# One-row DMAs by byte address, shared between SyncE and ScalarE, in the edge gathers of a four-layer graph network

## What is computed

```python
edge_index = jnp.stack([src, dst])
x = _layernorm(x + _L0_gnn_ref(x, edge_attr_2, src, dst, ...))        # softmax over edges, w * (z[src] + ez)
x = _layernorm(x + _L1_gnn_ref(x, edge_index))                        # segment_sum(x[src], dst)
x = _layernorm(x + _L2_gnn_ref(x, edge_index, edge_attr_16, ...))     # attention MLP on every edge, softmax, GRU
x = _layernorm(x + _L3_gnn_ref(x, src, dst, W, b))                    # softmax over edges, h[src] * alpha
```

## Time and profile before

| | us |
|---|---|
| median of 3 runs | 11547.42 (11536.29 to 11568.89) |
| the profiled execution, its time | 11551.36 |
| its span in the trace | 11549.4 |
| POOL busy, share of the span | 8177.0, 71% |
| DVE busy | 5633.5, 49% |
| ACT busy | 2838.7, 25% |
| PE busy | 2429.9, 21% |

### The profile page before, as it was taken

How to read it: one execution, slowest core, us unless ns; L and a number is a source line. 1 busy time by engine, 2 the same in 40 slices (tenths; PEclk the granted TensorE clock), 3 DMA queues, 4 the chain that set the end, 5 groups by cost and what they waited for, 6 DMA issues and landing times. The chain is left out here.

```text
span 11549.4 us, 88417 instructions
## 1 busy us (share of the span) xinstructions
PE 2429.9 (21%) x11904; PEld 1958.6 (17%) x11904; DVE 5633.5 (49%) x13767; ACT 2838.7 (25%) x4017; POOL 8177.0 (71%) x8465
## 2 busy tenths in 40 slices
PE   2322333332000000000000001666666630000000
PEld 2211323222000000000000001555555420000000
DVE  9999888882422222411111112777777642222223
ACT  0165555551211111122222210111111231111111
POOL 0076777777777777777777777777777667777776
PEclk8555555555555555555555555888888755555555
DMA  7011111012222222222222221333333212222222
GB/s 227 11 13 13 13 14 15 7 15 50 64 57 57 55 57 57 49 54 54 53 54 54 54 51 46 86 87 88 86 87 88 64 32 56 55 56 56 56 56 50
DMA packets 711039, 633.45 MB, mean 55 GB/s; under 512 B 476828, under 2 KB 534837, under 8 KB 709423
## 3 DMA queue, kind: packets, MB, share of 16 engines
q0 software_dynamic: 270464, 237.81, 12.7%
q1 hardware_dynamic: 390732, 224.72, 6.9%
q10 hardware_dynamic: 49248, 165.27, 3.7%
HBM read 322.30 MB, written 304.83 MB: 54 GB/s over the span
## 5 line engine op out<-in xcount | busy, mean ns | idle before, releaser
L1235 POOL DMA_INDIRECT l_rows<-table,l_sources x4623 | 4385.9, 949 | 1446.4 <-issue 1409.0
L632 POOL DMA_INDIRECT e_rows<-in_rec,base x1504 | 1530.7, 1018 | 1092.8 <-DVE marks L761 642.7
L1235 POOL DMA_INDIRECT l_pair<-table,l_slab x1568 | 1503.6, 959 | 483.0 <-issue 458.0
L1459 DVE TENSOR_TENSOR_SCAN l_totals<-l_factor,banks 128x510 f32<-128x510 f32 (+3 forms) x672 | 752.6, 1162 | 1638.4 <-ACT banks L1616 1637.4
L1626 ACT COPY l_kept<-l_totals 128x476 f32<-128x476 f32 (+3 forms) x672 | 639.3, 967 | 2990.6 <-DVE l_totals L1459 2980.6
L1390 DVE TENSOR_TENSOR l_score<-l_rows,base 128x14 f32<-128x14 f32 x224 | 44.4, 198 | 2590.4 <-DMA l_rows<-table,l_sources 2590.3
L1576 PE MATMUL banks<-ident,l_kept 128*65 128x128 f32 (+2 forms) x4 | 1.9, 464 | 5756.1 <-DVE junk L1508 5756.1
L1576 PEld LDWEIGHTS banks<-ident,l_kept 128*65 128x65 f32 (+2 forms) x4 | 0.7, 171 | 5758.2 <-DVE junk L1508 5758.2
L779 PE MATMUL banks<-marks 125*128 125x98 bf16 x3200 | 623.3, 366 | 1269.8 <-DVE marks L761 1269.8
L393 DVE COPY_PREDICATED area<-banks,area 128x2048 f32<-128x2048 int32 x342 | 869.4, 2597 | 0.2
L779 PEld LDWEIGHTS banks<-marks 125*128 125x128 bf16 x3200 | 459.9, 148 | 1420.7 <-DVE marks L761 1316.4
(11 more groups left out here) (313 smaller groups left out, 6301.3 us busy)
## 6 DMA issues: line engine op xcount, KB each, us to landing
l_rows<-table SPq DMA_DIRECT2D x6784, 0.3 KB
l_rows<-table,l_sources POOLq DMA_INDIRECT x4623
l_rows<-table SPq DMA_DIRECT2D x3584, 0.2 KB
sums<-l_kept ACTq DMA_DIRECT2D x112, 476.0 KB, 3.0
sums<-l_kept SPq DMA_DIRECT2D x224, 231.0 KB, 3.4
sums<-l_kept ACTq DMA_DIRECT2D x112, 462.0 KB, 2.7
seeds<-late_rows SPq DMA_DIRECT2D x130, 392.0 KB
sums<-l_kept ACTq DMA_DIRECT2D x112, 448.0 KB, 2.6
```

The costliest lines, as they stand in the source:

```text
L632: GP.indirect_dma_start(e_rows[:, u, g, :], None, A["rec16"], bass.IndirectOffsetOnAxis(e_ids[:, s * G16 + g:s * G16 + g + 1], 0)).then_in ...
L1235: GP.indirect_dma_start(pair[:, u, g, 0:D] if gated else rows[:, u, g, :], None, table[l], bass.IndirectOffsetOnAxis(at, 0)).then_inc(rows ...
L1459: V.tensor_tensor_scan(flat(totals[:, s % 2, h, 0:n, :]), flat(factor[:, s % 2, 0:n, :]), flat(fresh[s % 2][h][:, 0:n, :]), 0.0, ALU.mult, ...
```

## The change

One-row DMAs now see table and target as bytes, and their address is a byte offset that needs no scaling by the sequencer: VectorE multiplies the node numbers once by the row's bytes (`alone_wide` for layers 0 and 3, `alone_slim` for 1 and, anew, 2). SP fetches one column in 46 in layers 0, 1 and 3 and, newly, one in 64 in layer 2. ACT, newly, fetches one in 56 in layers 0, 1 and 3: one part of 32 rows in each step, for a column six steps ahead (`ACT_LEAD`). Over the edge loops POOL's columns fall from 1543 to 1510 in layer 0, from 1540 to 1507 in layers 1 and 3, and from 1568 to 1545 in layer 2. `powers_of` and `of_group` take their semaphores from shared ones.

```diff
-            sp.dma_start(alone_ids[0:STEPS // 4 * (P // ALONE_EACH), :],
-                         for_alone[:, :, :, 4 * G - 1]).then_inc(alone_ids_in, 16)
-        ALONE_FIRST = {0: 3, 1: 0, 3: 0}
-        alone_at = lambda l, s: l in ALONE_FIRST and s % 4 == 3 and s // 4 >= ALONE_FIRST[l]
+        SP_STRIDE, SP_FIRST = {0: 46, 1: 46, 2: 64, 3: 46}, {0: 2, 1: 0, 2: 1, 3: 0}
+        ACT_STRIDE, ACT_FIRST, ACT_LEAD = 56, {0: 2, 1: 1, 3: 1}, 6
+        def fetch_row(eng, l, to, at, landed):
+            flat = byte_view(table[l].rearrange("n w -> (n w)"))
+            eng.dma_start(byte_view(to), flat[bass.ds(at, 4 * TWL[l])].rearrange("(o w) -> o w", o=1)).then_inc(landed, 16)
...
+                by_sp = {t: SP_STRIDE[l] * (t + 1) - 1 for t in range(SP_FIRST[l], W // SP_STRIDE[l])} if l in SP_FIRST else {}
+                by_act = {t: ACT_STRIDE * (t + 1) - 2 for t in range(ACT_FIRST[l], W // ACT_STRIDE)} if l in ACT_FIRST else {}
+                alone = set(by_sp.values()) | set(by_act.values())
...
-                        for g in range(cols_by_pool(s)):
+                        for g in range(G):
+                            if s * G + g in alone:
+                                continue
...
+                    if l == 0:
+                        flat = dsrc[0:NQ].rearrange("(i c) -> c i", c=W)
+                        load_places(sp, 0, W // SP_STRIDE[0], flat[SP_STRIDE[0] - 1::SP_STRIDE[0], :])
+                        load_places(sp, ACT_AT, W // ACT_STRIDE, flat[ACT_STRIDE - 2::ACT_STRIDE, :])
...
                     def fetch_alone(s, r, u):
+                        for t, c in by_sp.items():
+                            if gated and 0 <= s - c // G < P // ALONE_EACH:
+                                fetch_part(t, s - c // G)
+                            elif not gated and c // G == s:
+                                if s >= RING:
+                                    sp.wait_ge(*done(read_last, s - RING))
+                                for h in range(P // ALONE_EACH):
+                                    fetch_part(t, h)
-                    in_turn(STEPS, RING, [(0, load), (12, save)] if gated else [(0, fetch_alone)])
+                    in_turn(STEPS, RING, [(0, load), (12, save), (0, fetch_alone)] if gated else
+                            [(0, fetch_alone)])
...
+                    if l == 0:
+                        dve.wait_ge(alone_ids_in, 32)
+                        for q, n in ((0, W // SP_STRIDE[0]), (ACT_AT, W // ACT_STRIDE)):
+                            tl(V.tensor_scalar(alone_wide[q:q + n, :], alone_slim[q:q + n, :], 4.0 * TWL[0], None, ALU.mult))
+                            V.tensor_scalar(alone_slim[q:q + n, :], alone_slim[q:q + n, :], 4.0 * TWL[1], None, ALU.mult
+                                            ).then_inc(alone_scaled, 1)
...
+                    def fetch_alone(s, r, u):
+                        for t, c in by_act.items():
+                            h = s - (c // G - ACT_LEAD)
+                            if 0 <= h < P // ALONE_EACH:
+                                if h == 0 and c // G >= RING:
+                                    act.wait_ge(*done(read_last, c // G - RING))
+                                at = row_places(l, mybir.EngineType.Activation, ACT_AT + t, h)
+                                for i in range(ALONE_EACH):
+                                    p = h * ALONE_EACH + i
+                                    fetch_row(act, l, rows[p:p + 1, c // G % RING, c % G, :], at[i],
+                                              act_rows_in[(t - ACT_FIRST[l]) % 2])
...
-                        in_turn(STEPS, RING, [(1, keep), (1, save), (0, scan_weight)] if soft else
-                                [(0, take_rows), (1, keep), (1, save)])
+                        in_turn(STEPS, RING, [(1, keep), (1, save), (0, scan_weight), (0, fetch_alone)] if soft else
+                                [(0, take_rows), (1, keep), (1, save), (0, fetch_alone)])
```

More of the change, by code:

```diff
@@ L1126, in build, with row_places, load_places @@
         sources_in = sem("sources_in")
-        ALONE_FIRST = {0: 3, 1: 0, 3: 0}
-        alone_at = lambda l, s: l in ALONE_FIRST and s % 4 == 3 and s // 4 >= ALONE_FIRST[l]
-        alone_ids_in = sem("alone_ids_in")
+        SP_STRIDE, SP_FIRST = {0: 46, 1: 46, 2: 64, 3: 46}, {0: 2, 1: 0, 2: 1, 3: 0}
+        ACT_STRIDE, ACT_FIRST, ACT_LEAD = 56, {0: 2, 1: 1, 3: 1}, 6
+        ACT_AT = P // 2
+        alone_ids_in, alone_scaled = sem("alone_ids_in"), sem("alone_scaled")
+        alone_at_byte = [alone_wide, alone_slim, alone_slim, alone_wide]
+        byte_view = lambda a: a.bitcast(mybir.dt.uint8)
+        def fetch_row(eng, l, to, at, landed):
+            flat = byte_view(table[l].rearrange("n w -> (n w)"))
+            eng.dma_start(byte_view(to), flat[bass.ds(at, 4 * TWL[l])].rearrange("(o w) -> o w", o=1)).then_inc(landed, 16)
+        def row_places(l, engine, q, h):
+            _, at = nc.values_load_multi_w_load_instructions(
+                alone_at_byte[l][q:q + 1, h * ALONE_EACH:(h + 1) * ALONE_EACH], [engine], min_val=0,
+                max_val=(NODES - 1) * 4 * TWL[l],
+                skip_runtime_bounds_check_because="source nodes of real and padded places are under NODES")
+            return at
+        def load_places(sp, q, n, words):
+            with nc.allow_non_contiguous_dma(reason="single words of a few columns, once"):
+                sp.dma_start(alone_slim[q:q + n, :], words).then_inc(alone_ids_in, 16)
         def edge_layer(l, k, kind, got, extra=None, first_do={}, node_stage=None):
@@ L1258, in edge_sync @@
                         sp.dma_start(sources[:], dsrc[0:NQ].rearrange("(p c) -> p c", p=P)).then_inc(sources_in, 16)
[L1259 to L1264 removed]
+                    first_do.get("sync", nothing)(sp)
+                    if l == 0:
+                        flat = dsrc[0:NQ].rearrange("(i c) -> c i", c=W)
+                        load_places(sp, 0, W // SP_STRIDE[0], flat[SP_STRIDE[0] - 1::SP_STRIDE[0], :])
+                        load_places(sp, ACT_AT, W // ACT_STRIDE, flat[ACT_STRIDE - 2::ACT_STRIDE, :])
+                    if gated:
+                        flat = rec_s[0:NQ, RE - 1:RE].bitcast(I32).rearrange("(i c) w -> c (i w)", c=W)
+                        load_places(sp, 0, W // SP_STRIDE[l], flat[SP_STRIDE[l] - 1::SP_STRIDE[l], :])
                     if soft:
@@ L1287, in save @@
                                      kept[:, s % KR, :, :]).then_inc(saved[s % KR].sem, 16)
-                    def fetch_alone(s, r, u):
-                        if not alone_at(l, s):
-                            return
-                        if s >= RING:
-                            sp.wait_ge(*done(read_last, s - RING))
-                        for h in range(P // ALONE_EACH):
-                            q = s // 4 * (P // ALONE_EACH) + h
-                            _, at = nc.values_load_multi_w_load_instructions(
-                                alone_ids[q:q + 1, :], [mybir.EngineType.SP], min_val=0, max_val=NODES - 1,
-                                skip_runtime_bounds_check_because="source nodes of real and padded places are under NODES")
-                            for i in range(ALONE_EACH):
-                                p = h * ALONE_EACH + i
-                                sp.dma_start(rows[p:p + 1, u, G - 1, :], table[l][bass.ds(at[i], 1), :]
-                                             ).then_inc(alone_in[s // 4 % 2], 16)
@@ L1305, in edge_sync, with fetch_part @@
-                    if not gated and l == 0:
-                        sp.wait_ge(alone_ids_in, 16)
-                    in_turn(STEPS, RING, [(0, load), (12, save)] if gated else [(0, fetch_alone)])
+                    def fetch_part(t, h):
+                        c = by_sp[t]
+                        at = row_places(l, mybir.EngineType.SP, t, h)
+                        for i in range(ALONE_EACH):
+                            p = h * ALONE_EACH + i
+                            to = pair[p:p + 1, c // G % RING, c % G, 0:D] if gated else rows[p:p + 1, c // G % RING, c % G, :]
+                            fetch_row(sp, l, to, at[i], sp_rows_in[(t - SP_FIRST[l]) % SP_SEMS].sem)
```

49 lines of the change are left out of this document (36 added, 13 removed).

## The result

| | before | after |
|---|---|---|
| median, us (7 runs each) | 11550.14 (11536.29 to 11568.89) | 11588.06 (11577.82 to 11591.1) |
| ratio | 1 | 1.0031, 95% interval 1.002 to 1.0043 |
| span of the profiled run | 11549.4 | 11580.5 |

What follows compares the result with a forecast made beforehand. POOL's gathers were taken to bound the edge loops, with ACT becoming layer 1's bound. From 11551.4 us: -41 + 29 - 13 - 41 + 1.5 = -65, so 11487, as median 11482; range 11395 to 11600 us.

Steps and rivals of the forecast that it cites:

- POOL bounds, 1.25 us per column; -41 in layers 0 and 3: Edge loops run at POOL's gather pace; 33 columns less save 41 us each in layers 0 and 3.
- SP's part of 13.1 us: SP's 32 one-row fetches plus register load, layers 0, 1, 3: pitch falls from 0.409 to 0.333 us, part to 13.1.
- The rival that the register operation was free: Only its own 37 ns or less go; SP parts 14.5 us, ACT 14.7, total 11800 and more; chance 0.07.
- No lock between SP and ACT: Both issue DMAs side by side; the rival that they block each other gives above 12500 us, chance 0.05.
- ACT's part x = 13.3 us: ACT's 32 fetches with register load, taken from SP's rows; layer 1 step 17.75 us against POOL's 16.8, layer +29 us.
- the 13.8 at which I let it join: ACT part length in us above which layer 0 also becomes ACT-bound, adding 104 us per us of part.
- Layer 2, a stall of 0.5 us per column: POOL waits for `turned` about 0.5 us per SP column; 23 columns gain 17, say 13 us.
- The lead of 45.2: Layer 2: SP's load for a step precedes that step's POOL gathers by 45.2 us, read at step 100.
- the feedback: Layer 2: stalls affect SP's next load; allowed for by lowering the gain from 17 to 13 us.
- four parts of 13.7 us: Layer 2 bound: with SP parts this long the gain is nothing; with no stall it is 29 us.
- The rest: VectorE's multiplications cost 1 us in layer 0, 0.5 in layer 2; added waits and semaphores change nothing.
- Its chance of ending slower: Whole kernel: slower by more than 0.3% given 0.23, the same 0.13, faster 0.64.

Runs made afterwards that it cites:

- g3: The change with ACT's fetches in layer 1 moved ahead of `keep` and `save`: 11482.31 us, ratio to before 0.9922.
- e7c: The change with ACT's layer 1 fetches ahead of `keep` and `save`, and SP issuing two parts in each of two layer 2 steps: 11398.63 us, 0.9872 of before.
- g2: The change without SP's fetches in layer 2, where POOL takes those 23 columns: 11562.43 us, ratio to before 0.9995.
- f1: The change with parts of 18 rows instead of 32 and fewer SP and ACT columns, results wrong: 11407.17 us, 0.9882 of before.
- e7: Same two reorderings as e7c against the change, run on a chip where everything was slower: 16350.84 us, 0.9462 of before.

## Why the prediction was wrong

Point by point, by the prediction's own steps:

- **POOL bounds, 1.25 us per column; -41 in layers 0 and 3:** right, -42 and -41.
- **SP's part of 13.1 us:** right. The pitch is 0.32 us in the middle and 0.334 to 0.339 in the mean, the part 13.0 to 13.2. The rival that the register operation was free is out.
- **No lock between SP and ACT:** right. Both stream side by side at 228 and 235 ns for whole layers. The rule of the Trainium skill ("Perfetto Trace Analysis", "DMA Instruction — HWDGE (DVE, Sync)") that the generator is locked for one sequencer's exclusive use isn't borne out for these two engines: the trace disagrees, though its section is headed for DVE and Sync and doesn't name ScalarE. In the change 7284 of SP's DMAs in layers 0, 1 and 3 were issued while ACT's went out beside them, at 0.332 us from one to the next in the mean; one after another the two would need 0.228 + 0.235 = 0.463 us.
- **ACT's part x = 13.3 us: the term that failed in layer 1, in its size.** The mechanism was as forecast: ACT becomes the bound, its own share of the step is 4.45 us (18.20 less a part of 13.74), it never waits for rows, POOL waits for stores at the end (90.7 us, forecast 70). But x was 13.74, at 107 us per us of x: 107 x 0.44 = +47, and +29 + 47 = +76 is what was measured. The DMAs have no part in these 0.44 us: 235 ns instead of 228 were allowed for with 6 ns each, and a part without its load took 10.9 us where the forecast has 13.3 - 2.17 = 11.1. It is the register load, 2.89 us for the 2.17 that I carried over from SP. I took it for a property of the instruction; g3 and e7c show that it depends on how lately a store of 128 partitions was issued. Behind one-row DMAs, or 1.3 us and more behind the store, it takes 2.2 us; right behind the store 2.6 on SP and 2.9 on ACT. SP's rows of before could not show it, since SP never loaded registers behind such a store. In layer 0 the part was 13.87, above the 13.8 at which I let it join, and it did not: the rest of the step is 2.60, not 2.8.
- **Layer 2, a stall of 0.5 us per column: the step that failed, by more than its bounds.** The mean of the 23 is 72.9 / 23 = 3.2 us. By the prediction's own terms, in the mean of the 23: the load is 44.1 us ahead of POOL instead of 45.2; from the load to the end of the last evacuation are 62.8 us instead of 62.0; from there to POOL's next gather 0.8, which I had put at nothing; and POOL is there at 16.3 instead of 16.4. With the forecast's 0.4 that makes 0.4 + 1.1 + 0.8 + 0.8 + 0.1 = 3.2. The lead of 45.2 came from a single step; the 23 steps of before that answer to the late ones have 43.2 to 46.9, in the mean 45.0, and step 100 had 43.2 even then. What the late columns do to the lead shows in the two groups: 43.8 us and a wait of 3.5 for the 19 that come nine steps behind another, 45.6 and 1.7 for the other four. In the 19 the `message` that the load waits for begins 29.5 us after its step's gathers, where before it was 25. So the feedback is worth some 1.7 us in 19 columns of 23; I had seen it and put it at 0.2 (13 for 17). And without it a column would still have cost 1.7 us for the 1.25 saved. The gain of 23 x 1.25 = 29 turns into a loss of 42 by the last gather, 37 over the layer. One bound was wrong in the prediction's own terms: four parts of 13.7 us instead of 13.1 come 2.4 us later, a stall of 2.8 and a loss of some 35 us; "nothing" is reached at 13.3.
- **The rest**, multiplications, added waits, semaphores: nothing is seen of it. With g2 layer 2 is 2299 us, not longer than before.

Both misses have one shape: two strings of work within 6% of each other (17.75 for 16.8 in layer 1, 16.8 for 16.4 in layer 2), and a fixed small overrun multiplied by the number of steps. That the range held the time is in part luck: at the measured x the prediction's own sum is -18 us, and the rest to +31 came from layer 2, for which it had no case of loss. Its chance of ending slower was too small.

What stays open is why a register load is longer behind a store, and why one-row DMAs go out at half the rate on some chips; both are only described here.

## What to carry to other kernels

When work is given to an engine that has slack on average, add up its string within one step, in program order, and compare it with the bound's step; where they are within some 6%, look for an order that lets the sequencer's work run beside the engine's own (here the same fetches ahead of `keep` and `save` turned +76 us into -43). Where a late result delays the one who feeds the next round, the lead of the undisturbed trace is too long, and the lead of one step is not the mean of all. And a duration carried over from another place is good only with the same neighbours at the same distance.

## What the runs showed of the hardware

- A load of 32 registers takes 2.2 us behind one-row DMAs and 2.6 (SP) or 2.9 us (ACT) right behind the issue of a 128-partition store; on ACT it is back at 2.2 when it begins 1.3 us or more after that issue (e7c). A load of 18 registers was uneven and in the middle longer: on SP 1.55 to 5.02 us, median 3.3, on ACT 2.19 to 5.20, median 3.6 to 3.7 (f1).
- A sequencer loads registers and issues DMAs while its engine still copies (e7c: copies from 5815.15 to 5816.90, the fetches from 5817.42, the load before them).
- SP and ACT issue one-row DMAs side by side at 228 and 235 ns with no sign of one holding the other up: SP's follow each other at 0.332 us in the mean beside ACT's and at 0.346 without them (the change).
- The same program took 11548 to 11569 us on some chips and 17163 to 17286 on others. In e7 SP's one-row DMAs are there 0.62 us apart in the mean (0.34 in the change), though the median length (228 ns) and the median distance (0.32 us) are unchanged: two thirds of the time lie in the third of the distances that are above 0.5 us.
